# The context of an attention layer turned by DMA transposes, pair of heads by pair of heads, kept whole on chip and projected from there

## What is computed

```python
latents = x @ W_down.T                       # 64 wide
keys, values = latents @ W_uk.T, latents @ W_uv.T
scores = einsum('bhqd,bhkd->bhqk', q, k) / sqrt(128)   # causal
ctx = einsum('bhqk,bhkd->bhqd', softmax(scores), v)
x = x + ctx.transpose(0, 2, 1, 3).reshape(b, s, h * dh) @ W_o.T
```

## Time and profile before

| | |
|---|---|
| Time, median of 3 runs | 266.6 us (266.31 to 267.62) |
| Span of the profiled execution | 264.7 us |
| TensorE / VectorE / ScalarE / GpSimd busy | 94% / 81% / 67% / 27% |
| Mean granted TensorE clock | 0.994 |
| Attention, steady part, per pair of heads | 16.2 us |
| From the last step but one of attention to the second mixture | 31.4 us |
| Second mixture of experts to the end | 33.9 us |

### The profile page before, as it was taken

One profiled execution on the slowest core, in us unless ns is written; L12 is line 12 of the kernel. 1 busy time (PEld: TensorE's weight loads), 2 busy tenths in 40 slices (PEclk: granted clock), 3 DMA queues, 4 the chain that ended last, 5 costly groups with the idle time before them and its releaser, 6 DMA issues.

```text
span 264.7 us, 7738 instructions
## 1 busy us (share of the span) xinstructions
PE 247.8 (94%) x2755; PEld 189.5 (72%) x2778; DVE 214.8 (81%) x507; ACT 176.1 (67%) x330; POOL 70.5 (27%) x124
## 2 busy tenths in 40 slices
PE   6899897999799999999999999999988999999996
PEld 2754366966668878788886887878876999854355
DVE  2877689996879989999899999999995444578783
ACT  2646770394878979888788897888884333445750
POOL 5130144000004443444343552534550000300310
PEclk9799999999999999999999999999999999999999
DMA  6999000001103011030110302102000000000004
GB/s 228 247 299 357 14 4 0 0 2 40 42 0 74 11 40 40 0 79 0 40 40 10 69 0 49 30 21 59 0 2 2 0 0 2 2 0 1 0 4 159
DMA packets 17832, 13.02 MB, mean 49 GB/s; under 512 B 8524, under 2 KB 17560, under 8 KB 17560
## 3 DMA queue, kind: packets, MB, share of 16 engines
q1 hardware_dynamic: 16616, 11.62, 17.2%
q10 hardware_dynamic: 1200, 1.18, 1.3%
HBM read 7.55 MB, written 1.05 MB: 32 GB/s over the span
## 4 chain that ended last, share of the span: by engine, by line
PE 69%; DVE 19%; ACT 4%; issue 3%; DMA 2%; POOL 1%; ACTq 0%; DVEq 0%
PE bank L847 17%; PE bank L1062 12%; PE bank L875 7%; PE bank L1053 7%; PE bank L1052 4%; PE bank L1076 3%; PE bank L970 3%; PE bank L1075 3%; PE bank L1138 3%; PE bank L1077 3%; PE bank L1009 3%; DVE pT_lo L732 2%; PE bank L1054 2%; DMA w1n<-in_L_ffn_w_dram 2%; DVE nmax L727 2%
## 5 line engine op out<-in xcount | busy, mean ns | idle before, releaser
L469 ACT ACTIVATE prob<-bank,nmax 128x384 f32<-128x384 f32 (+3 forms) x128 | 62.2, 527 | 8.2 <-DVE nmax L723 6.8
L732 DVE TENSOR_TENSOR pT_lo<-bank,pT_hi 128x512 f16<-128x512 f32 x80 | 54.5, 682 | 3.1 <-ACT pT_hi L475 2.4
L475 ACT CAST pT_hi<-bank 128x512 f16<-128x512 f32 x80 | 46.7, 584 | 11.1 <-PE bank L1062 10.6
L1062 PE MATMUL bank<-ident,prob 128*128 128x128 f32 x320 | 50.5, 280 | 0.6 <-ACT prob L469 0.6
L357 POOL TENSOR_TENSOR cst<-craw,rsum 128x256 f32<-128x256 f32 x30 | 18.4, 612 | 94.6 <-DVE craw L741 94.6
L1075 PE MATMUL bank<-lat,pT_hi 128*128 128x65 bf16 x320 | 37.7, 193 | 1.6 <-DVE pT_lo L732 1.6
L1076 PE MATMUL bank<-lat,pT_hi 128*128 128x64 bf16 x320 | 37.8, 195 | 0.0
L1053 PE MATMUL bank<-latT_lo,wqo 128*128 128x384 bf16 (+3 forms) x128 | 36.6, 299 | 1.2
L1077 PE MATMUL bank<-lat,pT_lo 128*128 128x65 bf16 x320 | 37.4, 192 | 0.0
L1075 PEld LDWEIGHTS bank<-lat,pT_hi 128*128 128x128 f16 x320 | 30.1, 96 | 6.5 <-issue 1.4
L1062 PEld LDWEIGHTS bank<-ident,prob 128*128 128x128 f32 x320 | 33.6, 140 | 0.8 <-issue 0.8
(11 more groups left out here) (183 smaller groups left out, 509.6 us busy)
## 6 DMA issues: line engine op xcount, KB each, us to landing
wqo<-stage SPq DMA_DIRECT2D x64, 64.0 KB, 2.0
wqo<-in_L_attn_W_q_dram SPq DMA_DIRECT2D x1, 2048.0 KB, 9.7
wqo<-in_L_attn_W_o_dram SPq DMA_DIRECT2D x1, 2048.0 KB, 14.5
out_dram<-X SPq DMA_DIRECT2D x8, 128.0 KB, 1.8
X<-in_L_attn_x_dram ACTq DMA_DIRECT2D x1, 512.0 KB, 7.0
wuk<-in_L_attn_W_uk_dram SPq DMA_DIRECT2D x1, 512.0 KB, 10.7
wuv<-in_L_attn_W_uv_dram SPq DMA_DIRECT2D x1, 512.0 KB, 9.7
w3n<-in_L_ffn_w_dram SPq DMA_DIRECT2D x1, 384.0 KB, 5.4
```

The costliest lines, as they stand in the source:

```text
L469: last = nc.scalar.activation(prob[:, u % 2, cols], bank[SCORE_BANK[u]][:, cols], ACT.Exp, bias=nmax[:, u, n:n + 1])
L475: nc.scalar.copy(pT_hi[:, j % 2, :], bank[3 + j % 2][:, :]).then_inc(pThi_ready, 1)
L732: nc.vector.tensor_tensor(pT_lo[:, j % 2, :], bank[3 + j % 2][:, :], pT_hi[:, j % 2, :], ALU.subtract).then_inc(pTlo_ready, 1)
L1062: last = nc.tensor.transpose(bank[3 + j % 2][:, blk(k)], prob[:, j % 2, blk(k)], ident[:, :])
```

## The change

Turning the context is taken from TensorE. A new buffer `cT` holds the whole turned context: 8 pairs x 2 parts x 8 blocks x 128 tokens, of 16 bits, on 128 partitions (32 KB in each). To make room for it, buffers that are used only before or after (`w1n`, `w3n`, `w2n`, `wuk`, `wuv`, `hT_hi`, `hT_lo`) are laid into the same bytes. `c_hi` and `c_lo` are ordered by pair first.

SyncE issues the transposes, two for each pair (high and low part), 262,144 bytes each. Its loop is written out. Those of pair `i - 2` stand behind the moves of the queries of pair `i`; those of pair 6 and of pair 7 (pair 7 in two halves of the tokens, so two times two of 131,072 bytes) stand behind them all. TensorE makes the last context without a break. It then projects pairs 0 to 5 of blocks 0 to 3, waits for pair 6 and for sequence 0 of pair 7, projects these, waits for the rest and projects blocks 4 to 7, with a bank of its own for nearly every block.

```diff
+        cT = sb("cT", [P, NP, 2, NB, P], BF16)
...
+            def transpose_context(i, first, until, done):
+                for part, c in enumerate((c_hi, c_lo)):
+                    sp.dma_start_transpose(cT[:, i, part, first:until, :],
+                                           c[:, i, first:until, :].rearrange("p n c -> p (n c)")).then_inc(done, 16)
+            for i in range(NP):
                 for t in range(2):
                     sp.wait_ge(u_lo, i * 2 + (t + 1))
...
+                if i >= 2:
+                    sp.wait_ge(clo_ready, B + 2 * B * (i - 1))
+                    transpose_context(i - 2, 0, NB, cT_early)
+            sp.wait_ge(clo_ready, B + 2 * B * (NP - 1))
+            transpose_context(NP - 2, 0, NB, cT_mid)
+            for b in range(B):
+                sp.wait_ge(clo_ready, B + 2 * B * (NP - 1) + b + 1)
+                sp.wait_ge(clo_last, b + 1)
+                transpose_context(NP - 1, SB * b, SB * (b + 1), cT_last[b])
...
-            def context_hi(r, waited):
-                act.wait_ge(cT_ps, waited)
-                nc.scalar.copy(stage[:, r, 0, :], bank[CTX_T_BANK[r][0]][:, :].bitcast(BF16)).then_inc(cThi_ready, 1)
...
-            def context_lo(r, waited):
-                dve.wait_ge(cThi_ready, waited)
-                nc.vector.tensor_copy(stage[:, r, 1, :], bank[CTX_T_BANK[r][1]][:, :].bitcast(BF16)).then_inc(cTlo_ready, 1)
...
+            for n in range(NB):
+                add_attention(n)
+                statistics(1, n, n + 1)
+                if n == HB - 1:
+                    aggregate(2, 0)
+                if n == HB:
+                    normalise_tokens(2, 0)
...
+            def project(n, first, until):
+                for i in range(first, until):
+                    for part, w in TERMS:
+                        last = mm(bank[OUT_BANK[n]][:, 0:D], cT[:, i, part, n, :], Nv[w][:, i, :],
+                                  start=(i == 0 and (part, w) == TERMS[0]), stop=(i == NP - 1 and (part, w) == TERMS[-1]))
...
+            for j in range(1, UNITS):
                 attention_step(NP - 1, j, with_queries=False)
...
+            pe.wait_ge(cT_early, 16 * 2 * (NP - 2))
+            for n in range(HB):
+                project(n, 0, NP - 2)
+            pe.wait_ge(cT_mid, 16 * 2)
+            pe.wait_ge(cT_last[0], 16 * 2)
+            for n in range(HB):
+                project(n, NP - 2, NP)
+            pe.wait_ge(cT_last[1], 16 * 2)
+            for n in range(HB, NB):
+                if n == NB - 1:
+                    transpose_xn(2, 0, 6)
+                if n == HB + 1:
+                    pe.wait_ge(x_added[1], 1)
+                project(n, 0, NP)
```

More of the change, by code:

```diff
@@ L108, in bass_macaron_moe_mla_moe, with within_cT @@
         h1c = ffn_buf[:, FC, :].rearrange("p (b n) -> p b n", b=2)
-        hT_hi = sb("hT_hi", [P, FC, T], BF16)
-        hT_lo = sb("hT_lo", [P, FC, T], BF16)
+        cT = sb("cT", [P, NP, 2, NB, P], BF16)
+        cT_flat = cT[:, :, :, :, :].rearrange("p i a n t -> p (i a n t)")
+        taken = [0]
+        def within_cT(size, dt):
+            at = taken[0]
+            taken[0] += size * (2 if dt == F32 else 1)
+            assert taken[0] <= NP * 2 * NB * P
+            piece = cT_flat[:, at:taken[0]]
+            return piece.bitcast(F32) if dt == F32 else piece
+        hT_hi = within_cT(FC * T, BF16).rearrange("p (j t) -> p j t", j=FC)
+        hT_lo = within_cT(FC * T, BF16).rearrange("p (j t) -> p j t", j=FC)
         lg = sb("lg", [P, NB, E], F32)
@@ L127, in bass_macaron_moe_mla_moe @@
         wgtT = sb("wgtT", [2 * E, T], BF16)
-        w1n = sb("w1n", [P, FC, D], F32)
-        w3n = sb("w3n", [P, FC, D], F32)
-        w2n = sb("w2n", [P, DC, EF], F32)
+        w1n = within_cT(FC * D, F32).rearrange("p (j d) -> p j d", j=FC)
+        w3n = within_cT(FC * D, F32).rearrange("p (j d) -> p j d", j=FC)
+        w2n = within_cT(DC * EF, F32).rearrange("p (c f) -> p c f", c=DC)
         gaten = sb("gaten", [E, D], F32)
@@ L159, in bass_macaron_moe_mla_moe @@
         lat = sb("lat", [P, NB, 2 * LAT + 1], BF16)
-        stage = sb("stage", [P, 2, 2, T], BF16)
+        stage = sb("stage", [P, 2, T], BF16)
         prob = sb("prob", [P, 2, SEQ], F32)
@@ L237, in bass_macaron_moe_mla_moe @@
         clo_last = sem("clo_last")
-        cT_ps = sem("cT_ps")
-        cThi_ready = sem("cThi_ready")
-        cTlo_ready = sem("cTlo_ready")
+        cT_early = sem("cT_early")
+        cT_mid = sem("cT_mid")
+        cT_last = [sem(f"cT_last{b}") for b in range(B)]
         attn_ps = sem("attn_ps")
@@ L352, in _, with divide_context @@
             pool.wait_ge(n_hi, 4)
-            with pool.Fori(0, H - 1) as h:
+            def divide_context(i, side):
                 for b in range(B):
-                    pool.wait_ge(rsum_ready, h * B + (b + 1))
-                    pool.wait_ge(ctx_free, h * B + (B + b + 1))
+                    of_head = slice(LAT * side, LAT * (side + 1))
+                    pool.wait_ge(rsum_ready, i * (2 * B) + (side * B + b + 1))
+                    pool.wait_ge(ctx_free, i * (2 * B) + (side * B + B + b + 1))
                     nc.gpsimd.tensor_tensor(cst[:, b, :, :], craw[:, b, :, :],
                                             rsum[:, b, :].unsqueeze(2).to_broadcast([P, SB, LAT]), ALU.mult).then_inc(cst_ready, 1)
[L359 to L363, removed]
+                    pool.wait_ge(cst_ready, i * (2 * B) + (side * B + b + 1))
+                    hi, lo = (c[:, bass.ds(i, 1), SB * b:SB * (b + 1), of_head].rearrange("p i n l -> p (i n) l") for c in (c_hi, c_lo))
+                    nc.gpsimd.tensor_copy(hi, cst[:, b, :, :]).then_inc(chi_ready, 1)
+                    pool.wait_ge(chi_ready, i * (2 * B) + (side * B + b + 1))
+                    nc.gpsimd.tensor_tensor(lo, cst[:, b, :, :], hi, ALU.subtract).then_inc(clo_ready, 1)
+            with pool.Fori(0, NP - 1) as i:
+                for side in range(2):
+                    divide_context(i, side)
+            divide_context(NP - 1, 0)
             ffn(1)
@@ L512, in split_last_context @@
                 act.wait_ge(ctx_free, (H - 1) * B + B + b + 1)
-                nc.scalar.copy(c_hi[:, SB * b:SB * (b + 1), (H - 1) * LAT:H * LAT], cst[:, b, :, :]).then_inc(chi_last, 1)
-            def context_hi(r, waited):
-                act.wait_ge(cT_ps, waited)
-                nc.scalar.copy(stage[:, r, 0, :], bank[CTX_T_BANK[r][0]][:, :].bitcast(BF16)).then_inc(cThi_ready, 1)
+                nc.scalar.copy(c_hi[:, NP - 1, SB * b:SB * (b + 1), LAT:2 * LAT], cst[:, b, :, :]).then_inc(chi_last, 1)
             split_last_context(0)
-            context_hi(0, 1)
             split_last_context(1)
-            with act.Fori(0, HB // 2) as i:
-                context_hi(1, i * 2 + 2)
-                context_hi(0, i * 2 + 3)
             layernorm_std(2, 0)
-            for n in range(HB + 1, NB):
-                context_hi(n % 2, n + 1)
             split_xT(1, 0)
@@ L1130, in _ @@
                     attention_step(i, j)
-            for j in range(1, UNITS - 1):
-                attention_step(NP - 1, j, with_queries=False)
[L1135 to L1167, removed]
+            TERMS = [(0, 0), (0, 1), (1, 0)]
+            def project(n, first, until):
[3 more added lines that the diff above has]
+                                  start=(i == 0 and (part, w) == TERMS[0]), stop=(i == NP - 1 and (part, w) == TERMS[-1]))
+                if until == NP:
+                    last.then_inc(attn_ps, 1)
```

50 lines of the change are left out of this document (14 added, 36 removed).

## The result

The changed kernel takes 258.17 us (median of 4 runs, 257.85 to 260.2) against 266.48 before (266.31 to 267.62): the ratio is 0.970, 95% interval 0.966 to 0.974, so 8 us faster. The forecast was 258.3.

The account below looks back on a forecast made before the run. TensorE alone was taken to bound the stretch from attention's end to the second mixture; 7.8 us of transposes and 0.4 to 0.5 of wait go, so 266.6 - 8.3 = 258.3 us, 8-in-10 range 257.0 to 301.0.

Parts of the forecast that it names:

- What bounds the stretch: Between attention's last steps and the second mixture, 31.4 us, only TensorE is full (30.3 us); removing copies alone gives nothing.
- The sum: Second mixture begins at 222.5 instead of 230.81: 8.3 us less, 7.8 of transposes and 0.4 to 0.5 of wait.
- What is late next: During projection, VectorE's adds, statistics and `xn` stay hidden, `xn` with 2.5 us of cover; the 33.9 us tail shifts unchanged.
- X: Time SyncE's queue spends on one 262,144-byte DMA transpose; taken as 2.3 us, with bounds 1.15 and 10.8.
- The turning point: Transposes at the end of SyncE's queue: deadlines hold up to X = 4.3; no gain is left at X = 5.8.
- the forecast's formula: For SyncE's queue with X above 5.8, the loss is 5 (2X - 11.65) + 6X - 34.8 = 16X - 93.
- the slower rival: SyncE's queue cannot keep up, X above 5.8: 285.6 us at X = 7, 346 at 10.8; chance 0.28.
- The queue that cannot keep up: Same as the slower rival: SyncE's queue overloaded by transposes, X above 5.8; chance 0.28, half of it above 302 us.
- Contention: Transposes slow engines' SBUF access in attention; 1.0 us on each of eight pairs eats the gain; chance 0.04.
- Element by element: DMA transposes split into 131,072 pieces, X = 295 and milliseconds in all; chance 0.01.

Follow-up runs that it names:

- the first form: Changed kernel with 14 copies of 128x512 out of PSUM put back on ScalarE and seven on VectorE, feeding nobody, VectorE's wait ahead of the `xn` transposes: 259.65 us.
- Doubling X: Changed kernel with every DMA transpose issued twice, the added one first and into a spare buffer: 261.1 us.
- tripling it: Changed kernel with every DMA transpose issued three times, two of them first and into spare buffers: 267.7 us.
- five times: Changed kernel with every DMA transpose issued five times, four of them first and into spare buffers: 303.71 us.
- the filled version: Changed kernel with 18 products of block 0 with pairs 0 to 5 moved ahead of the last two contexts, nine each: 256.99 us.

## Why the prediction was right

**What bounds the stretch.** Right, and shown from both sides: transposes back on TensorE take 7.3 of the 8.3 us back (265.8), copies back on the others at most 0.4.

**The sum.** 7.8 us of transposes and 0.4 to 0.5 of the wait ahead of block 0 were forecast, 8.3; the stretch gave 8.32. The last context waited for its probabilities as it was worked out (0.62 us in the row). Its 1.65 us for turning block 1 was taken over from the trace of before; why these 16 took longer than the others stays open.

**What is late next.** Nothing was. For `xn` 2.5 us of cover were forecast. In the changed kernel it is ready at 215.9 and turned from 218.55, which is 2.7:

```profile
214.51 1.38 DVE L593 TENSOR_SCALAR xn<-X,mv,rstd 128x256 f32<-128x256 f32 x4
```

With the added copies of the first form it was ready at 217.7 only, so this cover is thin.

**The size of X.** 2.3 us was taken for a whole transpose, 1.3 to 1.4 was measured. The count of pieces was right (256 bytes), their price was not: 1.4 x 16 / 1,024 is 22 ns of a DMA engine for one, not the 36 ns of the moves. Since everything up to 4.3 was said to be covered, the miss did not reach the time: that the total came out is owed to this wide cover and not to the value taken for X. Of the two pages of the Trainium skill that were weighed, the trace agrees with neither wholly. 262,144 bytes in 1.38 us, back to back, are 190 GB/s. That is under the 261 GB/s that the Trainium skill ("DMA: Bandwidth & Descriptors", "Latency and other measured facts") gives for a transpose with a non-contiguous middle dimension, a condition that the forecast left out. The Trainium skill ("VectorE: DVE Perf Modes", "The three transpose paths") gives 1309 ns for one block of 128x128. Here an instruction with two, four or eight blocks held SyncE for 1.25, 1.27 or 1.33 us, so multiplying that figure by eight was the wrong estimate. No run has an instruction with one block.

**The turning point.** This step failed, without being called upon. X was taken to grow with the bytes, so that the four half transposes at the end would cost 2X. They cost nearly 4X, being four instructions of 1.19 to 1.27 us, and one of them took 2.41. With X = 1.33 the forecast's own sum would have left 5.9 us at the end. The trace leaves 3.0: the last one is issued at 205.19 and lands about 2.5 later, at 207.7, where it is wanted at 210.7. Doubling X eats that (1.64 us of wait), tripling it brings the kernel back to before (267.7, of which 2.7 us are the low clock), where the forecast had put that at X = 5.8, four times the true one. Beyond it the forecast's formula let the queue lose only what the transposes take above the gap between two sets of moves. For five times, with X = 7.0, it gives 285.6 us; 303.7 was measured. So the slower rival was nearer than it looked.

**The rivals.** The queue that cannot keep up is real, but needs more than three times the price. Contention, priced at 1.0 us for a pair (0.3 in the expectation for the doubled transposes), did not show with the DMA share at 0.48. Element by element was wrong: the packets say so.

## What to carry to other kernels

Work that only rearranges data may leave a full TensorE for the DMA queue, and is then worth TensorE's time for it and for the waits that go with it, if each transfer is issued a stage ahead of its use. Count such DMAs by instruction on the issuing queue, together with what stands behind them there, and look at the last ones first: they have the least cover, and where TensorE waited 5 us or more in these runs it lost its clock as well. Once the operands are there early, look for the small waits of the stage before and fill them.

## What the runs showed of the hardware

- A DMA transpose within SBUF kept the issuing engine for 1.25 us at 64 KB, 1.27 at 128 KB and 1.33 at 256 KB, against 0.5 to 0.6 for one of the moves of 64 KB (medians before and after the change). It landed 2.4 us after its issue at the smaller sizes and about 3.3 at 256 KB. Here and there one took 2.0 to 2.5 us to issue; why stays open.
- TensorE's granted clock was at 0.50 (1.2 GHz) after idle times of 5.0, 8.6 and 18.8 us, which cost 1.8 to 2.7 us in the products behind. After idle times of 1.64 and 2.2 us it was at 1.00.
- The lower clock also showed at the program's start, in some executions only; what decides it stays open. The first 18 products of the first mixture took 3.99 us in one, 5.68 in another, with no difference in the code ahead. A stretch of each, of the changed kernel and of the same kernel run again, the granted clock standing ahead of the DMA share:

```profile
12.60:16.60 4.00, 4.00 (x21) 1.92 (x21) 2.97 (x9) 1.33 (x4) 1.67 (x5) 1.00 1.04 354
```

```profile
12.60:18.30 5.70, 5.70 (x21) 2.36 (x21) 3.26 (x10) 1.34 (x4) 1.41 (x5) 0.70 1.11 322
```

  That is 1.7 us, more than the filled version's whole gain, and most of the 2 us by which its runs and those of the changed kernel spread. A difference of that size is read from a stretch of the trace that leaves the start out, and not from the medians.
